# Attention in steps of two tiles: maximum, two score tiles, maximum, two mixes; GpSimd adds up eight or nine tiles of twelve

## The chip, the cores and the metric

The kernel runs on one core of one Trainium2 chip. The metric is the device time of one execution in microseconds; the time before is the median of three runs.

A core has five engines, each with its own stream of instructions: TensorE multiplies matrices (PE in the profile; PEld is its loading of weights), VectorE (DVE) and GpSimd (POOL) do elementwise work and VectorE reductions too, ScalarE (ACT) does activation functions and copies, and SyncE (SP) issues transfers. They run independently and wait for each other on semaphores only. Products land in PSUM; the rest lies in SBUF.

## The reference

Two transformer layers on `x`, 32 batches of 56 rows of 256, each with cross attention and then a mixture of experts. The change is in the attention alone. Its keys and values are the same 1500 rows of 64 of a batch (`ctx_512`) with rotary embedding; there are 16 heads. Per layer:

```
q_big = einsum('bshk,hkq->bshq', q_hk, w_kc_q)
kv_r = _apply_rope(kv_c, sin_k[None], cos_k[None])
q_r = einsum('bshq,hqr->bhsr', q_big, W_qr)
k_r = einsum('bld,hdr->bhlr', kv_r, W_kr)
scores = einsum('bhsr,bhlr->bhsl', q_r, k_r)
attn = softmax(scores, axis=-1)
ctx_c = einsum('bhsl,bld->bhsd', attn, kv_r)
ctx_lat = einsum('bhsd,hkd->bhsk', ctx_c, w_kc_kv)
```

## The kernel before

Each layer's attention goes through the 32 batches in four groups of eight (`BG`). A group begins with the projection of its queries (`qwide`, `query`); then come its batches one by one. The heads' queries are folded so that a batch has 896 query columns (16 heads of 56 rows), held as two halves of 448 on partitions 0 to 63 and 64 to 127; keys are held twice for that. The 1500 keys of a batch are 12 tiles of 125. The steps that matter, by the names that the schedule gives them:

- `smax` ("maximum"): a piece of the scores of a *later* batch (a quarter of the queries by a third of the keys), made only to find each query's maximum. TensorE writes it to the PSUM region `pair` (L853), VectorE reduces it to `maxpart` (L1120). A batch takes 12 of them, one for each tile of the batch before it. There is one `pair`, so a maximum is issued only when VectorE has drained the last one.
- `score`: a tile's scores in about full precision: `kparts` with `qhigh` (two products) and with `qlow` (L874), then the `shift` row that subtracts the maximum (L879). The two regions `wide` are taken in turn. ScalarE takes the exponential into `prob` (L975), which has four places.
- `mix`: `prob` times the values `kv` into one accumulator for the whole batch (L893). It is issued one tile late, after the next tile's scores. GpSimd adds the tiles' exponentials up in `sum_pool` (L1035, profile name `sums`) for the first `pool_tiles(b)` tiles; VectorE adds up the rest (L1141).
- `context`: after the last tile, ScalarE copies the accumulator (`ctx_raw`, L982) and VectorE adds its sum and GpSimd's (L1154).
- `norm`, `spread`, `share`: TensorE adds the sums over partitions (L900), ScalarE copies (`total`), the sums go by transfer to `packed`, VectorE takes the reciprocal (L1160), it goes to memory and back to all partitions (`zrec_merged`, `recip`), and VectorE multiplies (`ctx_n`, L1184).
- `maxneg`, `maxT`: the maxima of the next batch are reduced, transposed by TensorE (L859), copied by ScalarE and moved by transfer to `shift`; the first tile of the next batch waits for it.
- layer 0 only: `rotate` (GpSimd, L1007, L1008), `ropecos` (VectorE, `rope_c`, L1053), `rope` (VectorE, `kv`, L1063) and `keyT` (four transposes on TensorE, L811, a copy by ScalarE, a subtraction by VectorE to `kparts`, L1093) make the keys and values of a batch two or three ahead. Layer 1 fetches them.

`attention_schedule` writes all steps in one list, and every engine walks through that list and issues its part, waiting on semaphores. So the place of a step in the list is its place in the queue of every engine that takes part in it, SyncE's too.

Of the kernel before, what the change touches and what calls it, by code (L numbers as in the profile page):

```python
# [15 lines left out]
BG = 8  # L16
# [13 lines left out]
POOL_TILES, POOL_LAST = 11, 7  # L30
# [22 lines left out]
def pool_tiles(b):  # L53
    return POOL_TILES if b % BG < BG - 1 else POOL_LAST

def pool_sums(b):

    return sum(pool_tiles(i) - 1 for i in range(b))

def vector_sums(b):  # L60

    return sum(LT - pool_tiles(i) for i in range(b))

def attention_schedule(layer):
# [34 lines left out]
    for g in range(G):  # L99
        first, old = BG * g, BG * g - 1  # L100
        if layer == 0:
            for n in range(H + 1):
# [4 lines left out]
                if g and n == 0:  # L107
                    add("mix", old, LT - 1)
                    add("context", old)
# [39 lines left out]
        else:  # L149
            for p in range(NPAIR):  # L150
# [3 lines left out]
                if g and p == 0:  # L154
                    add("mix", old, LT - 1)
                    add("context", old)
# [26 lines left out]
        last = None  # L183
        for j in range(BG):
            b = first + j
            for t in range(LT):
                ahead = (j + 1, t + EARLY_MAX) if t + EARLY_MAX < LT else (j + 2, t + EARLY_MAX - LT)
# [4 lines left out]
                if layer == 0 and t == LT - 3 and b + 3 < NB:  # L192
                    add("rotate", b + 3)
# [24 lines left out]
                if layer == 0 and t >= LT - 2 and b + 3 < NB:  # L218
                    add("ropecos", b + 3, t - LT + 2)
                if layer == 0 and t in (1, 2) and b + 2 < NB:  # L220
                    add("rope", b + 2, t - 1)
                if g + 1 < G and j == BG - 2 and t == 4:
                    add("heads", g + 1)
                if g + 1 < G and j == BG - 1:
                    if t == 2:
                        add("mean", g + 1, region=3)
                    if t in (3, 4):
                        add("square", g + 1, t - 3)
                    if t == 5:
                        add("var", g + 1, region=3)  # L230
                    if t in (7, 8):
                        add("rstd", g + 1, t - 7)
                    if t == 9:
# [4 lines left out]
    add("mix", NB - 1, LT - 1)  # L238
# [373 lines left out]
def attention(nc, layer, a, scratch, x_all, sems, phase_range, sb, stack, region, c):  # L612
# [67 lines left out]
    with nc.Block() as block:  # L680
# [104 lines left out]
        def _(pe):  # L785
# [6 lines left out]
            for kind, key, reg in steps:  # L792
# [103 lines left out]
                elif kind == "norm":  # L896
                    b, = key
                    pe.wait_ge(s["dve_sum"], vector_sums(b + 1))
# [22 lines left out]
        def _(act):  # L921
            for kind, key, reg in steps:
# [40 lines left out]
                elif kind == "score":  # L963
# [3 lines left out]
                    if n_ >= NPROB:  # L967
# [3 lines left out]
                        if to < pool_tiles(bo):  # L971
                            act.wait_ge(s["pool_sum"], pool_sums(bo) + max(1, to))
                        else:
                            act.wait_ge(s["dve_sum"], vector_sums(bo) + max(1, to - pool_tiles(bo)))
# [16 lines left out]
        def _(pool):  # L991
            for kind, key, reg in steps:
# [16 lines left out]
                elif kind == "qrope":  # L1009
# [4 lines left out]
                    if g and h == 0:  # L1014
                        pool.wait_ge(s["dve_sum"], vector_sums(BG * g))
# [6 lines left out]
                elif kind == "mix":  # L1022
                    b, t = key
                    if 1 <= t < pool_tiles(b):
# [3 lines left out]
                        if t == 1:  # L1028
                            if b >= 2:
                                pool.wait_ge(s["dve_sum"], vector_sums(b - 1))  # L1030
                            first_in = prob[:, (n_ - 1) % NPROB, :]
                        else:
                            pool.wait_ge(s["pool_sum"], pool_sums(b) + t - 1)
# [4 lines left out]
        def _(dve):  # L1038
# [3 lines left out]
            for kind, key, reg in steps:  # L1042
# [52 lines left out]
                elif kind == "qrope":  # L1095
# [5 lines left out]
                    if g and h == 0:  # L1101

                        dve.wait_ge(s["premix"], LT * BG * g)
                        dve.wait_ge(s["pool_sum"], pool_sums(BG * g))
# [846 lines left out]
```

## Time and profile before

| | |
|---|---|
| median of three runs | 3254.75 us (3250.76 to 3263.74) |
| profiled execution, its own time | 3258.38 us |
| its span | 3256.6 us |
| TensorE, VectorE, ScalarE, GpSimd busy | 2906.2, 1959.9, 1184.5, 1660.3 us |
| layer 0's attention, about | 200 to 1460 us of the span |
| layer 1's attention, about | 1860 to 2900 us of the span |

The span is one profiled execution. An engine's busy share says how much it did, not what the others waited for; a busy TensorE can still be one that changes over between products. In the timeline, a line is one or several instructions of an engine, with what released it in brackets if the engine stood idle before.

### The profile page before, as it was taken

What the parts mean: (1) busy time and instruction counts of PE and PEld (TensorE: products, weight loads), DVE (VectorE), ACT (ScalarE), POOL (GpSimd) and SP (SyncE); (2) the same over time, 40 slices, a digit from 0 to 9 for tenths busy, and PEclk for the clock granted to TensorE, in tenths of its full rate; (3) what the DMA queues carried; (4) which work ended last, traced back from release to release, by engine and by line L of the source; (5) the groups of instructions that cost most, each with busy time, mean ns of one, the idle gap of its engine ahead of it and who ended that gap; (6) DMA issues with size and microseconds to landing.
All of it is one profiled execution on the core that took longest, in us unless ns stands there. A gap on an engine that the chain in (4) does not pass through costs nothing. (4 is left out here: it accounts for less than half of the span.)

```text
span 3256.6 us, 42708 instructions
## 1 busy us (share of the span) xinstructions
PE 2906.2 (89%) x15992; PEld 1650.1 (51%) x15992; DVE 1959.9 (60%) x2318; ACT 1184.5 (36%) x1644; POOL 1660.3 (51%) x947
## 2 busy tenths in 40 slices
PE   7689999998998999996899699899989989968888
PEld 6444444444544454445788444444444444436555
DVE  3476667666766676745766556556456566545553
ACT  3124441444144414443333244434424434422221
POOL 0367775776676657762100077567647737720000
PEclk9689999999999999998999799999999999988888
DMA  8333331333133413312000323223323313210000
GB/s 280 90 88 79 88 93 35 80 78 100 33 80 81 103 37 75 76 33 83 1 1 1 87 65 81 70 68 83 74 51 81 94 30 81 57 48 1 6 6 12
DMA packets 102326, 212.32 MB, mean 65 GB/s; under 512 B 30690, under 2 KB 77778, under 8 KB 94572
## 3 DMA queue, kind: packets, MB, share of 16 engines
q1 hardware_dynamic: 102124, 209.59, 24.8%
q8 instruction: 132, 2.16, 0.3%
q14 instruction: 70, 0.57, 0.1%
HBM read 138.51 MB, written 46.00 MB: 57 GB/s over the span
## 5 line engine op out<-in xcount | busy, mean ns | idle before, releaser
L1035 POOL TENSOR_TENSOR sums<-sums,prob 125x896 f32<-125x896 f32 x544 | 1148.2, 2111 | 207.9 <-ACT prob L975 160.6
L1120 DVE TENSOR_REDUCE maxpart<-pair 112x2 f32<-112x1000 f32 x720 | 861.0, 1196 | 468.4 <-PE pair L853 468.2
L975 ACT ACTIVATE prob<-wide 125x896 f32<-125x896 f32 x768 | 704.4, 917 | 874.0 <-PE wide L879 870.9
L893 PE MATMUL single<-prob,kv 125*64 125x448 f32 x3072 | 757.4, 572 | 0.7
L874 PE MATMUL wide<-qhigh,kparts 64*125 64x448 f32 x3072 | 455.0, 374 | 8.3 <-DVE maxpart L1120 8.3
L853 PE MATMUL pair<-kparts,qhigh 64*112 64x500 f32 x1440 | 349.4, 482 | 71.5 <-DVE maxpart L1120 70.3
L853 PEld LDWEIGHTS pair<-kparts,qhigh 64*112 64x112 f32 x1440 | 126.2, 172 | 493.1 <-DVE maxpart L1120 422.5
L1035 POOL TENSOR_TENSOR sums<-prob 125x896 f32<-125x896 f32 x64 | 134.7, 2105 | 457.9 <-ACT prob L975 457.9
L874 PEld LDWEIGHTS wide<-qhigh,kparts 64*125 64x125 f32 x3072 | 278.5, 184 | 116.5 <-issue 78.2
L879 PE MATMUL wide<-shift,ones_row 64*125 64x448 f32 x1536 | 286.1, 367 | 10.0 <-DMA shift<-maxrow 9.9
L874 PE MATMUL wide<-qlow,kparts 64*125 64x448 f32 x1536 | 284.2, 365 | 0.0
L893 PEld LDWEIGHTS single<-prob,kv 125*64 125x64 f32 x3072 | 153.2, 136 | 240.7 <-issue 235.5
L996 POOL TENSOR_TENSOR w_low<-w_low_values,w_high 128x384 fp32r<-128x384 f32 (+1 forms) x96 | 98.4, 1031 | 305.2 <-ACT w_high L941 305.2
L1752 POOL TENSOR_TENSOR ffn_hsum<-ffn_hid 128x448 f32<-128x448 f32 (+1 forms) x24 | 27.9, 1161 | 297.2 <-DVE ffn_hid L1878 297.2
L1020 POOL TENSOR_TENSOR sums<-prob 96x448 f32<-96x448 f32 x128 | 145.8, 1160 | 47.3 <-issue 24.1
L879 PEld LDWEIGHTS wide<-shift,ones_row 64*125 64x125 f32 x1536 | 145.4, 184 | 27.2 <-DMA shift<-maxrow 13.9
L874 PEld LDWEIGHTS wide<-qlow,kparts 64*125 64x125 f32 x1536 | 144.6, 184 | 13.6
L788 PE MATMUL wide<-x_high,w_high 128*96 128x448 f32 (+1 forms) x320 | 126.1, 394 | 21.3 <-POOL w_low L996 13.6
L1184 DVE TENSOR_TENSOR ctx_n<-ctx_raw,recip 128x448 f32<-128x448 f32 x62 | 91.2, 1472 | 84.2 <-DMA recip<-zrec_merged 84.2
L913 PE MATMUL wide<-ctx_n,wvo 128*128 128x448 f32 x256 | 121.5, 631 | 6.7 <-DVE ctx_n L1176 4.3
L1093 DVE TENSOR_TENSOR kparts<-single,kparts 64x500 fp32r<-64x500 f32 x94 | 63.0, 670 | 97.4 <-ACT kparts L948 97.4
L789 PE MATMUL wide<-x_high,w_low 128*96 128x448 f32 (+1 forms) x320 | 119.0, 372 | 0.0
(319 smaller groups left out, 3882.2 us busy)
## 6 DMA issues: line engine op xcount, KB each, us to landing
kparts<-keys_merged SPq DMA_DIRECT2D x64, 750.0 KB, 8.8
kparts<-kparts SPq DMA_DIRECT2D x96, 250.0 KB, 3.1
keys_merged<-kparts SPq DMA_DIRECT2D x32, 750.0 KB, 7.3
recip<-zrec_merged SPq DMA_DIRECT2D x124, 112.0 KB, 2.8
w_low_values<-w_merged SPq DMA_DIRECT2D x64, 192.0 KB, 2.4
raw<-in_ctx SPq DMA_DIRECT2D x32, 375.0 KB
values_merged<-kv SPq DMA_DIRECT2D x32, 375.0 KB
kv<-values_merged SPq DMA_DIRECT2D x32, 375.0 KB
```

Source lines behind the costliest of these rows:

```text
L788: pe.matmul(dst, w_hi, x_hi, start=start, stop=False)
L789: pe.matmul(dst, w_lo, x_hi, start=False, stop=False)
L853: mm = pe.matmul(acc[0:TQ, half, 0:LB], qhigh[rows_of(half), b % BG, t * TQ:(t + 1) * TQ], kparts[rows_of(half), b % 3, 0, third * LB:(thi ...
L874: pe.matmul(acc[0:LP, half, 0:HQ], kparts[rows_of(half), b % 3, part, cols], q[rows_of(half), b % BG, :], start=(i == 0), stop=False)
L879: mm = pe.matmul(acc[0:LP, half, 0:HQ], c["ones_row"][rows_of(half), 0:LP], shift[rows_of(half), b % 2, :], start=False, stop=True)
L893: mm = pe.matmul(mix_acc[64 * half:64 * half + DC, 0:HQ], kv[:, b % 3, t, :], prob[:, (b * LT + t) % NPROB, half * HQ:(half + 1) * HQ], st ...
L913: mm = pe.matmul(attn_acc[:, m, 0:NT].rearrange("p (j s) -> p j s", j=BG), wvo[:, i, m * 128:(m + 1) * 128], ctx_n[:, :, i * S:(i + 1) * S ...
L975: nc.scalar.activation(prob[:, n_ % NPROB, :].rearrange("p (a b) -> p a b", a=2), acc[0:LP, :, 0:HQ], ACT.Exp)\
L996: nc.gpsimd.tensor_tensor(w_low[:, h % HSLOT, :, :], w_in[:, h % HSLOT, :, :], w_high[:, h % HSLOT, :, :].bitcast(F32), ALU.subtract)\
L1020: nc.gpsimd.tensor_tensor(qr[:, h % 4, half, :], qa[:, h % 2, half, :], qb[:, h % 2, 1 - half, :], ALU.add)\
L1035: nc.gpsimd.tensor_tensor(dst, first_in, prob[:, n_ % NPROB, :], ALU.add).then_inc(s["pool_sum"], 1)
L1120: V.tensor_reduce(maxpart[:, b % 2, t:NMAX:4, third], acc[0:TQ, :, 0:LB], AX.X, ALU.max).then_inc(*R.signal_drained(kind, *key))
```

## The change

The loop over tiles becomes a loop over steps of two tiles. A step issues a maximum, both tiles' scores, a second maximum, and then both mixes of the step before. What hung on odd tiles moves: `norm` from tile 1 to step 2, `maxT` from tile 9 to step 8 (and so ahead of `spread` in the list), both `rope` adds to step 2, `keyT` from tiles 3, 4, 5 to steps 4, 6, 10, `rotate` to step 8, both `ropecos` and `stash` to step 10. VectorE's adding gets a kind of its own, `sum`, of the step's own tiles rather than at the mix. GpSimd takes 8 tiles in layer 0 and 9 in layer 1 where it took 11 (the last batch of a group keeps 7); VectorE takes the others.

```diff
-POOL_TILES, POOL_LAST = 11, 7
+POOL_TILES, POOL_LAST = (8, 9), 7
...
-            for t in range(LT):
-                ahead = (j + 1, t + EARLY_MAX) if t + EARLY_MAX < LT else (j + 2, t + EARLY_MAX - LT)
...
-                add("score", b, t, region=t % 2)
+            for t in range(0, LT, 2):
+
+                ahead = [(j + 1, u + EARLY_MAX) if u + EARLY_MAX < LT else (j + 2, u + EARLY_MAX - LT) for u in (t, t + 1)]
...
                 if j + 1 < BG and t == 8:
                     add("maxneg", b + 1)
-                if last is not None:
-                    add("mix", *last)
-                    if last[1] == LT - 1:
-                        add("context", last[0])
-                last = (b, t)
-                if t == 1 and j:
+                if ahead[0][0] < BG:
+                    maximum(first + ahead[0][0], ahead[0][1])
+                for u in (t, t + 1):
+                    add("score", b, u, region=u % 2)
+                if ahead[1][0] < BG:
+                    maximum(first + ahead[1][0], ahead[1][1])
+                if before is not None:
+                    for u in range(2):
+                        add("mix", before[0], before[1] + u)
+                    if before[1] == LT - 2:
+                        add("context", before[0])
+                before = (b, t)
+                for u in (t, t + 1):
+                    add("sum", b, u)
+                if t == 2 and j:
                     add("norm", b - 1, region=3)
-                if j + 1 < BG and t == 9:
+                if j + 1 < BG and t == 8:
                     add("maxT", b + 1, region=3)
-                if layer == 0 and t in (3, 4, 5) and b + 2 < NB:
-                    add("keyT", b + 2, t - 3, region=3)
-                if layer == 0 and t == LT - 1 and b + 2 < NB:
-                    add("stash", b + 2)
-                if ahead[0] < BG:
-                    maximum(first + ahead[0], ahead[1])
+                if layer == 0 and b + 2 < NB:
+                    places = (4, 6, 10) if j + 1 < BG else (6, 8, 10)
+                    if t in places:
+                        add("keyT", b + 2, places.index(t), region=3)
+                    if t == 10:
+                        add("stash", b + 2)
+                    if t == 2:
+                        for part in range(2):
+                            add("rope", b + 2, part)
+                if layer == 0 and b + 3 < NB:
+                    if t == 8:
+                        add("rotate", b + 3)
+                    if t == 10:
+                        for part in range(2):
+                            add("ropecos", b + 3, part)
                 if t == 8 and j:
                     add("spread", b - 1)
                 if t == 10 and j:
                     add("share", b - 1, 2)
```

In VectorE's stream, one batch in the middle of layer 0, from the sum of the batch before to that of this one, was this (`maxpart` are the reductions of maxima; an x2 is two in a row):

```order
L1154 TENSOR_TENSOR sums<-prob,sums 125x896
L1120 TENSOR_REDUCE maxpart<-pair 112x2 x2
L1063 TENSOR_TENSOR kv<-rope_c,rope_s 125x384
L1120 TENSOR_REDUCE maxpart<-pair 112x2
L1063 TENSOR_TENSOR kv<-rope_c,rope_s 125x384
L1093 TENSOR_TENSOR kparts<-single,kparts 64x500
...
L1160 RECIPROCAL packed_recip<-packed 112x8
L1120 TENSOR_REDUCE maxpart<-pair 112x2 x2
L1184 TENSOR_TENSOR ctx_n<-ctx_raw,recip 128x448
L1053 TENSOR_TENSOR rope_c<-raw,cosk 125x384
L1120 TENSOR_REDUCE maxpart<-pair 112x2
L1053 TENSOR_TENSOR rope_c<-raw,cosk 125x384
```

and becomes this:

```order
L1171 TENSOR_TENSOR sums<-sums 125x896
L1137 TENSOR_REDUCE maxpart<-pair 112x2 x2
L1080 TENSOR_TENSOR kv<-rope_c,rope_s 125x384 x2
L1137 TENSOR_REDUCE maxpart<-pair 112x2 x2
...
L1137 TENSOR_REDUCE maxpart<-pair 112x2 x2
L1158 TENSOR_TENSOR sums<-sums,prob 125x896 x2
L1110 TENSOR_TENSOR kparts<-single,kparts 64x500
L1070 TENSOR_TENSOR rope_c<-raw,cosk 125x384 x2
L1201 TENSOR_TENSOR ctx_n<-ctx_raw,recip 128x448
L1137 TENSOR_REDUCE maxpart<-pair 112x2 x2
```

The work between reductions is gathered behind every second one, and two `sums` join it at the batch's end.

TensorE's stream in layer 1, around the norm, was this (`single` takes the mixes and the norm):

```order
L879 MATMUL wide<-shift,ones_row 125x448 x2
L893 MATMUL single<-prob,kv 64x448 x2
L900 MATMUL single<-sums,ones 64x448 x2
L853 MATMUL pair<-kparts,qhigh 112x500 x2
L874 MATMUL wide<-qhigh,kparts 125x448 x4
L874 MATMUL wide<-qlow,kparts 125x448 x2
L879 MATMUL wide<-shift,ones_row 125x448 x2
L893 MATMUL single<-prob,kv 64x448 x2
L853 MATMUL pair<-kparts,qhigh 112x500 x2
```

and becomes this:

```order
L870 MATMUL pair<-kparts,qhigh 112x500 x2
L891 MATMUL wide<-qhigh,kparts 125x448 x4
L891 MATMUL wide<-qlow,kparts 125x448 x2
L896 MATMUL wide<-shift,ones_row 125x448 x2
L891 MATMUL wide<-qhigh,kparts 125x448 x4
L891 MATMUL wide<-qlow,kparts 125x448 x2
L896 MATMUL wide<-shift,ones_row 125x448 x2
L870 MATMUL pair<-kparts,qhigh 112x500 x2
L910 MATMUL single<-prob,kv 64x448 x4
L870 MATMUL pair<-kparts,qhigh 112x500 x2
```

Two tiles' scores stand between two maxima, and two mixes behind the second.

SyncE's transfers of a batch of layer 1 were in this order:

```order
L759 DMA packed<-total 56x1x8 x2
L736 DMA kparts<-keys_merged 64x3000 x2
L738 DMA kv<-values_merged 125x768
L763 DMA zrec_merged<-packed_recip 112x8
L768 DMA recip<-zrec_merged 64x448 x2
L777 DMA shift<-maxrow 1x4x112 x2
```

and become:

```order
L753 DMA kparts<-keys_merged 64x3000 x2
L755 DMA kv<-values_merged 125x768
L776 DMA packed<-total 56x1x8 x2
L794 DMA shift<-maxrow 1x4x112 x2
L780 DMA zrec_merged<-packed_recip 112x8
L785 DMA recip<-zrec_merged 64x448 x2
```

The shift transfers now stand ahead of those of the reciprocals.

## Rows read from the trace of the kernel before

**Rows 1.** The page, busy time and share of TensorE.

```profile
PE 2906.2 (89%) x15992; PEld 1650.1 (51%) x15992; DVE 1959.9 (60%) x2318; ACT 1184.5 (36%) x1644; POOL 1660.3 (51%) x947
```

**Rows 2.** Timeline, one tile of layer 1: start, length, engine, line, operation.

```profile
2217.64 0.48 PE L853 MATMUL pair<-kparts,qhigh 64*112 64x500 f32 x2
...
2217.83 20.08 POOL L1035 TENSOR_TENSOR sums<-sums,prob 125x896 f32<-125x896 f32 x9 [0.78 <-ACT prob L975]
...
2217.95 0.56 PE L874 MATMUL wide<-qhigh,kparts 64*125 64x448 f32 x4
2218.15 1.20 DVE L1120 TENSOR_REDUCE maxpart<-pair 112x2 f32<-112x1000 f32 x1 [0.94 <-PE pair L853]
...
2218.35 0.36 PE L874 MATMUL wide<-qlow,kparts 64*125 64x448 f32 x2
...
2218.55 0.37 PE L879 MATMUL wide<-shift,ones_row 64*125 64x448 f32 x2
...
2218.85 0.97 PE L893 MATMUL single<-prob,kv 125*64 125x448 f32 x4
2218.96 0.92 ACT L975 ACTIVATE prob<-wide 125x896 f32<-125x896 f32 x1 [1.21 <-PE wide L879]
...
2219.75 0.48 PE L853 MATMUL pair<-kparts,qhigh 64*112 64x500 f32 x2
```

**Rows 3.** Timeline, end of a batch in layer 1 and its norm.

```profile
2210.16 1.28 DVE L1184 TENSOR_TENSOR ctx_n<-ctx_raw,recip 128x448 f32<-128x448 f32 x1 [0.56 <-DMA recip<-zrec_merged]
...
2212.47 1.08 DVE L1154 TENSOR_TENSOR sums<-prob,sums 125x896 f32<-125x896 f32 x1
2212.61 0.48 PE L853 MATMUL pair<-kparts,qhigh 64*112 64x500 f32 x2 [0.40 <-DVE maxpart L1120]
...
2213.83 0.97 PE L893 MATMUL single<-prob,kv 125*64 125x448 f32 x4
...
2214.64 0.92 PE L900 MATMUL single<-sums,ones 125*64 125x448 f32 x4
...
2215.49 0.48 PE L853 MATMUL pair<-kparts,qhigh 64*112 64x500 f32 x2
```

**Rows 4.** Timeline, end of a batch in layer 0.

```profile
608.78 0.54 DVE L1053 TENSOR_TENSOR rope_c<-raw,cosk 125x384 f32<-125x384 f32 x1
...
610.49 0.48 PE L853 MATMUL pair<-kparts,qhigh 64*112 64x500 f32 x2 [1.97 <-DVE maxpart L1120]
```

**Rows 5.** Windows: stretch, length, busy per engine, granted clock, DMA share, GB/s.

```profile
611.40:614.80 3.40, 3.40 (x12) 0.77 (x8) 1.61 (x2) 0.92 (x1) 1.78 (x1) 0.50 0.31 79
...
579.30:768.00 188.70, 171.27 (x1102) 84.01 (x1102) 124.19 (x132) 83.59 (x108) 137.94 (x72) 0.98 0.33 84
```

**Rows 6.** Timeline, transfers of reciprocals and shift, and the shift's late landing.

```profile
2205.29 0.32 SPq L763 DMA_DIRECT2D zrec_merged<-packed_recip  x1
...
2207.82 1.35 SPq L777 DMA_DIRECT2D shift<-maxrow  x2
...
2320.09 0.62 DVE L1184 TENSOR_TENSOR ctx_n<-ctx_raw,recip 128x448 f32<-128x448 f32 x1 [8.87 <-DMA recip<-zrec_merged]
2320.10 0.46 PE L879 MATMUL wide<-shift,ones_row 64*125 64x448 f32 x2 [2.12 <-DMA shift<-maxrow]
```

**Rows 7.** Timeline, VectorE and GpSimd adding at once at the end of a group.

```profile
461.96 4.08 POOL L996 TENSOR_TENSOR w_low<-w_low_values,w_high 128x384 fp32r<-128x384 f32 x3 [1.95 <-ACT w_high L941]
...
462.44 1.43 DVE L1184 TENSOR_TENSOR ctx_n<-ctx_raw,recip 128x448 f32<-128x448 f32 x1
```

**Rows 8.** Timeline, key transposes in layer 0.

```profile
619.99 0.59 PE L811 MATMUL single<-ident,kv 125*64 125x125 f32 x4 [0.67 <-DVE kv L1063]
...
620.51 0.48 PE L853 MATMUL pair<-kparts,qhigh 64*112 64x500 f32 x2
...
621.23 0.67 DVE L1093 TENSOR_TENSOR kparts<-single,kparts 64x500 fp32r<-64x500 f32 x1 [1.39 <-ACT kparts L948]
...
621.83 1.18 DVE L1120 TENSOR_REDUCE maxpart<-pair 112x2 f32<-112x1000 f32 x1
```

More of the change, by code:

```diff
@@ L51, in head_at, with pool_tiles, pool_sums, vector_sums @@
     return n // 2 + n % 2 * NPAIR
[L53 to L62, printed above, removed]
+def pool_tiles(layer, b):
+    return POOL_TILES[layer] if b % BG < BG - 1 else POOL_LAST
+def pool_sums(layer, b):
+    return sum(pool_tiles(layer, i) - 1 for i in range(b))
+def vector_sums(layer, b):
+    return sum(LT - pool_tiles(layer, i) for i in range(b))
 def attention_schedule(layer):
@@ L107, in attention_schedule @@
                 if g and n == 0:
-                    add("mix", old, LT - 1)
+                    for u in range(2):
+                        add("mix", old, LT - 2 + u)
                     add("context", old)
@@ L154, in attention_schedule @@
                 if g and p == 0:
-                    add("mix", old, LT - 1)
+                    for u in range(2):
+                        add("mix", old, LT - 2 + u)
                     add("context", old)
@@ L203, in attention_schedule @@
-                last = (b, t)
-                if t == 1 and j:
+                if ahead[0][0] < BG:
[5 more added lines that the diff above has]
+                if before is not None:
+                    for u in range(2):
+                        add("mix", before[0], before[1] + u)
+                    if before[1] == LT - 2:
+                        add("context", before[0])
@@ L224, in attention_schedule @@
                 if g + 1 < G and j == BG - 1:
+                    if t == 0:
+                        add("mean", g + 1, region=3)
                     if t == 2:
[L226 to L229, printed above, removed]
+                        for k in range(KT):
+                            add("square", g + 1, k)
+                    if t == 4:
                         add("var", g + 1, region=3)
-                    if t in (7, 8):
-                        add("rstd", g + 1, t - 7)
-                    if t == 9:
+                    if t == 6:
+                        for part in range(2):
+                            add("rstd", g + 1, part)
+                    if t == 8:
                         add("xsplit", g + 1)
@@ L237, in attention_schedule @@
                             add("wsplit", g + 1, n)
-    add("mix", NB - 1, LT - 1)
+    for u in range(2):
+        add("mix", NB - 1, LT - 2 + u)
     add("context", NB - 1)
@@ L897, in _ @@
                     b, = key
-                    pe.wait_ge(s["dve_sum"], vector_sums(b + 1))
+                    pe.wait_ge(s["dve_sum"], vector_sums(layer, b + 1))
                     for half in range(2):
@@ L1014, in _ @@
                     if g and h == 0:
[L1015 removed]
+                        pool.wait_ge(s["dve_sum"], vector_sums(layer, BG * g))
                         pool.wait_ge(*R.filled("norm", BG * g - 1))
@@ L1023, in _ @@
                     b, t = key
-                    if 1 <= t < pool_tiles(b):
+                    if 1 <= t < pool_tiles(layer, b):
                         pool.wait_ge(*R.drained("score", b, t))
@@ L1127, in _ @@
                     V.tensor_reduce(maxneg[:, b % 2, 0:NMAX], maxpart[:, b % 2, :, :], AX.X, ALU.max, negate=True).then_inc(s["maxneg"], 1)
-                elif kind == "mix":
+                elif kind == "sum":
                     b, t = key
-                    if t > pool_tiles(b):
+                    if t > pool_tiles(layer, b):
                         n_ = b * LT + t
@@ L1133, in _ @@
                         dst = sum_dve
-                        if t == pool_tiles(b) + 1:
+                        if t == pool_tiles(layer, b) + 1:
                             if b:
@@ L1145, in _ @@
                     other = sum_dve
-                    if vector_sums(b + 1) - vector_sums(b) == 1:
+                    if vector_sums(layer, b + 1) - vector_sums(layer, b) == 1:
                         dve.wait_ge(*R.drained("score", b, LT - 1))
```

28 lines of the change are left out of this document (11 added, 17 removed).

## The prediction

> **What bounds the kernel now.** I read the page first: TensorE is busy 89% of the span [rows 1]. The page's share says nothing of which wait ends last, so I went to the timeline of the two attention stages, which hold 64 batches of 12 tiles. In one tile of layer 1 at full clock [rows 2] TensorE never stands idle: maximum to scores 0.31 us, scores 0.40 + 0.20, shift to mix 0.30, mix to the next maximum 0.90; a tile takes 2.11. Two of these steps are dearer than the streaming in them. A mix followed by work of its own shape hands over after 0.81 (2213.83 to 2214.64), and the norm, the same shape as a mix, hands over to a maximum after 0.85 [rows 3]. So each change between "64 rows at a time" products (maximum, scores) and "64 columns at a time" products (mix) costs time, and now there are two changes per tile.
>
> VectorE is the second thing to look at, because there is one maximum buffer: a maximum can be issued only when the reduction of the one before is done. The reduction starts 0.51 us after the maximum and takes 1.20 [rows 2], so a maximum is free 1.77 us after the last one, if VectorE does nothing else in between. At the end of a batch it does: `ctx_n` and `sums` stand between two reductions, and TensorE waits 0.40 us in layer 1 [rows 3] and 1.97 us in layer 0 [rows 4]. After that wait the granted clock is 0.50, that is 1.2 instead of 2.4 GHz, for 3.4 us [rows 5]. Over six batches of layer 0 the mean clock is 0.98 [rows 5].
>
> **TensorE's part of the change.** Per two tiles: 0.31, 0.60 (first scores), 0.20, 0.60 (second), 0.20, second maximum 0.31, first mix 0.81, second mix 0.85 = 3.88 us, against 4.22. The two handovers of 0.20 (scores to scores, scores to maximum) are not in the trace; I take the 0.20 between `qlow` and `shift` products of one shape [rows 2]. The other bound is 0.31, as from maximum to scores, which has the same shape too: then it is 4.10. Maximum to mix I take at 0.31 for the same reason. Saved: 0.34 us for each of the 320 two-tile steps that have maxima (40 of the 48 steps of each group of eight batches; the last eight have no batch left to look ahead to), -109 us; in the 64 without, twice 0.90 + 0.60 + 0.30 = 3.60 becomes 0.60 + 0.20 + 0.60 + 0.30 + 0.81 + 0.85 = 3.36, -15. Together -124 (bounds -46 and -124).
> The Trainium skill (TensorEngine Tiling, Key Properties) says that changing the tiling mode drains TensorE, while tiles within a mode run on. Rows 2 and 3 agree: 0.90 against 0.81. By that rule alone, with nothing else on the way, the sum would end here, at about 3,130 us.
>
> **VectorE's part.** The second maximum of a step is wanted 1.92 us after the first (0.31 + 0.60 + 0.20 + 0.60 + 0.20), the next step's first 1.96 us later. With a reduction of 1.20 starting 0.51 in, the free time between two reductions is 0.72 and 0.76 us. Everything else that VectorE does now stands in one of six places per batch, behind the second reduction of a step, and what is longer than about 0.9 us there holds TensorE up, since the maximum after next waits for it. Instructions follow each other 0.1 us before the profile's end of the one before, so a reduction counts 1.12, a lone `sums` (1.08 [rows 3]) 1.0; two that depend on each other count 2.1.
> *End of a batch, layer 1.* Counted from the first maximum of step 10: second reduction 2.43 to 3.55, two `sums` to 5.7, `ctx_n`, next reduction. `ctx_n` needs the reciprocals. From issue of `zrec_merged` (2205.29) to the start of `ctx_n` (2210.16) it is 4.87 us [rows 3, 6]; that issue now stands behind the two shift transfers, which take 1.35 to issue [rows 6] and wait for the maxT at the end of step 8. That puts the issue at 5.8 and `ctx_n` at 10.7 from the start of step 8, or 6.6 from step 10. Then `ctx_n` 0.54 (GpSimd has ended its eight sums by then), the reduction 7.1 to 8.3, and the maximum that was wanted at 5.8 goes at 8.4: a stall of 2.6 against 0.4 now, 20 times; 1.1 in each of 4 first batches, that have no `ctx_n`. +48 us.
> *End of a batch, layer 0.* Behind the reduction stand two `sums` (2.1), `kparts` (0.60 [rows 8]), two `rope_c` (0.47 each [rows 4]) and `ctx_n` (0.54): the next reduction starts at 7.75, the maximum wanted at 6.3 goes at 9.0. 2.7 against 1.97, 20 times, and 2.2 against nothing, 4 times: +23 us.
> *The two `kv` adds, layer 0, step 2.* They read two SBUF tensors, and so does GpSimd's sum. The timeline shows what these do to each other [rows 7]: of three `w_low` on GpSimd the first runs while `ctx_n` waits for it, the second only after `ctx_n`: 4.08 us for the three, and 1.43 for a `ctx_n` that takes 0.62 when GpSimd is not in the way [rows 6]. The first `kv` comes at 3.55. In step 2 GpSimd has tile 2 from 2.4 to 4.5 us and tile 3 ready behind it (tile 2's exponential ends at 0.91 + 0.41 + 0.92; sums go 20.08 / 9 = 2.23 apart [rows 2]). The first `kv` gets through at 4.9, GpSimd takes the next 2.1, the second `kv` ends at 7.4, and the maximum wanted at 6.5 goes at 8.6: 2.1 us, 27 batches, +57. What goes away is the 0.67 that the transposes waited for `kv` [rows 8], -18.
> *The key transposes in steps 4 and 6.* `kparts` starts 0.72 us after the maximum behind the transposes was issued and the reduction at 1.32 [rows 8] where 0.51 is usual; now the 2.11 us of a tile and the 0.52 of the transposes lie between that maximum and the next and hide it; with 1.92 between them 0.65 us show. 51 of them, +33.
> The Trainium skill (SBUF — State Buffer, on the shared port pair) says that VectorE and GpSimd hold this pair for a whole instruction and the other one fully blocks. Rows 7 show just that. It speaks against this change where it gives VectorE more adds of two SBUF tensors, 3 a batch instead of 1 in layer 1, but I find GpSimd idle at the places of those.
>
> **The clock.** Of the 20 waits of about 2.0 us that layer 0 has at ends of batches, the mean clock of 0.98 says that 8 or so were followed by a fall (0.02 / 0.5 x 189 us = 7.5 us at half clock per six batches, 3.4 us each [rows 5]). A fall costs 1.7 us. The changed kernel has 27 waits of 2.1 us and 40 of 2.6 or 2.7: at the same share 11 and 16 falls, 19 more than now, +32 (bounds 0, if waits in another rhythm cause no more than now, and +73, if each of the 40 causes one).
> **The shift row.** In batch 6 of a group the transfers of the next group's weights delay the reciprocals, and the shift transfer queued behind them lands late: TensorE waits 2.12 us [rows 6]. Now shift goes first. 6 times, -13.
> **GpSimd.** Sums are 2.23 apart [rows 2], more than the 1.94 a tile would take. With 7 or 8 of them per batch, not 10, it ends before the batch does; this I cost at nothing. With 10 it would set the pace.
>
> **Sum**, against the profiled execution (3258.4 us, span 3256.6): -124 + 48 + 23 + 57 - 18 + 33 + 32 - 13 = +38, so 3296; the median of the three runs is 3.6 below that execution, which gives 3293. The first term has a size of which I am sure within its bounds, the stalls in the few places that I could walk through; rounded, I forecast **3290 us**, 1.1% slower.
>
> **Rivals.**
> *Faster: the `kv` adds are not parted* (0.22). If GpSimd doesn't come between them, or if its third sum isn't ready, the second `kv` ends at 5.4 and the stall is 0.1. That takes 54 us and 11 falls (19 us) off: 3217. It decides the sign once fewer than half of the 27 batches show the second `kv` waiting. For it: VectorE's instructions follow without a gap, so VectorE may keep its place. Against: the turns in [rows 7].
> *No change: the clock stays* (0.25). All stalls come, yet TensorE falls no more often than now: 3258. For it: 12 of the 20 waits of 2.0 us had no fall behind them. Against: 8 had.
> *Slower still: GpSimd gets in before `ctx_n`* (0.10). Its first sum of the next batch becomes ready 0.4 us after `ctx_n` starts. If the reciprocals come later than that, `ctx_n` waits for a sum, 1.8 us in 40 batches: 3362. For it: a margin of 0.4 us at the end of a chain of 5. Against: that chain was steady enough for a wait of 0.56 only [rows 3].
> *The change doesn't do what it says* (0.08). Handovers within one shape cost 0.31: +78, 3368. For it: maximum to scores has one shape and costs 0.31. Against: `qlow` to `shift`, 0.20.
> *Forecast* (0.35): 3260 to 3320.
>
> "Faster", "same" and "slower" are parted at 0.5%, about what a measurement of this kernel can tell from no change (3238 and 3271). Faster: the first rival and a little of the second, 0.25. Same: the rest of the second and the low end of the forecast, 0.26. Slower 0.49. For eight in ten the range takes in the `kv` rival at its centre and leaves out most of the two dear ones: 3205 to 3335; the likeliest case alone is 3260 to 3320.
>
> **What would show it.** Right: two-tile steps of 3.9 us on TensorE with mixes 0.8 + 0.85; waits of the maximum for `maxpart` of 2.6 to 2.7 us once a batch and, in layer 0, of about 2 us after the `kv` adds, of which the second is some 2.5 us long; a lower mean clock in layer 0 than 0.98; no wait for `shift` in batch 6. Wrong: a second maximum that goes on time after `ctx_n`, layer 1 batches clearly under 26 us, `kv` adds of 0.55 back to back, or ScalarE waiting for sums, which would mean that GpSimd sets the pace after all.

## The result, and the profile after

The changed kernel takes 3320.34 us (median of 4 runs, 3316.98 to 3338.34), the kernel before, run on the same chip beside it, 3254.05 us (3250.76 to 3263.74). The ratio is 1.0209, 95% interval 1.0184 to 1.0233: slower by 2%, 66 us. Forecast were 3290 us and a range of 3205 to 3335, so the side and the range held; the size was 30 us short, 66 us of loss where some 35 were forecast, and the time lies at the upper end of the likeliest case (3260 to 3320).

The head of the page, and the page's first line on TensorE, answer to [rows 1]:

```profile
span 3316.0 us, 42706 instructions
...
PE 2844.9 (86%) x15992; PEld 1733.0 (52%) x15992; DVE 2145.9 (65%) x2458; ACT 1147.2 (35%) x1644; POOL 1369.1 (41%) x807
```

TensorE is busy 61.3 us less than before (2906.2), and the span is 59.4 us longer (3256.6 before): it stands idle for 471.1 us where it stood for 350.4. The clock hides a part of the saving. These are the views of the cores, first of before, then of after (span, mean granted clock):

```profile
core 0: 3256.6 us, clock 0.948
```

```profile
core 0: 3316.0 us, clock 0.932
```

The clock has only the levels 0.50 and 1.00 in these traces, so TensorE was at 1.2 GHz for (1 - 0.948) x 2 x 3256.6 = 339 us before and for (1 - 0.932) x 2 x 3316.0 = 451 us after. Half of the 112 us more, 56, is streaming that took twice as long. So the 59.4 us are made of three parts: 117 less work at full clock, 121 more idle, 56 lost to the clock. Not all of the last is the change's: 79 of the 112 us at half clock lie between the first and the last copy of an accumulator (`ctx_raw`) in each layer, 24 lie ahead of the first one (14 of these before any attention, in the first 200 us), and 10 behind the last one. In that first part the other kernels with the new order have between 3 us less and 29 us more than the one before, so how much of the 24 the change makes is open.

Whom TensorE waits for stands in the view of waits, after and, where the front shows none, before (line, releaser: total us, times, longest):

```profile
PE pair L870 <- DVE maxpart L1137: 221.8, 154, 4.8
```

```profile
PE pair L853 <- DVE maxpart L1120: 70.3, 84, 2.0
```

151 us of waiting for one reduction have come. Some 28 us of other waits have gone (19 for `kv`, 9 for `shift`), which leaves about the 121 us of idle time more. What stands between the reductions is seen in the timeline of the changed kernel, first at the end of a batch in layer 1, from the first maximum of the step before the last. It answers to [rows 2, 3]:

```profile
2252.86 0.48 PE L870 MATMUL pair<-kparts,qhigh 64*112 64x500 f32 x2
...
2254.79 0.39 PE L870 MATMUL pair<-kparts,qhigh 64*112 64x500 f32 x2
2255.11 0.20 PEld L910 LDWEIGHTS single<-prob,kv 125*64 125x64 f32 x4 [0.30 <-ACT prob L992]
...
2256.95 0.48 PE L870 MATMUL pair<-kparts,qhigh 64*112 64x500 f32 x2
...
2257.34 1.29 SPq L794 DMA_DIRECT2D shift<-maxrow  x2
...
2258.68 0.44 SPq L780 DMA_DIRECT2D zrec_merged<-packed_recip  x1
...
2260.45 1.08 DVE L1158 TENSOR_TENSOR sums<-prob 125x896 f32<-125x896 f32 x1
2260.87 0.17 PEld L870 LDWEIGHTS pair<-kparts,qhigh 64*112 64x112 f32 x2 [0.70 <-DVE maxpart L1137]
...
2261.63 1.09 DVE L1158 TENSOR_TENSOR sums<-sums,prob 125x896 f32<-125x896 f32 x1
...
2263.53 0.63 DVE L1201 TENSOR_TENSOR ctx_n<-ctx_raw,recip 128x448 f32<-128x448 f32 x1 [0.81 <-DMA recip<-zrec_merged]
2264.01 2.09 POOL L1052 TENSOR_TENSOR sums<-prob 125x896 f32<-125x896 f32 x1 [5.52 <-ACT prob L992]
2264.07 1.19 DVE L1137 TENSOR_REDUCE maxpart<-pair 112x2 f32<-112x1000 f32 x1
...
2265.32 0.48 PE L870 MATMUL pair<-kparts,qhigh 64*112 64x500 f32 x2 [2.35 <-DVE maxpart L1137]
```

`sums`, `sums`, a wait for the reciprocals, `ctx_n`, and only then the reduction: the maximum goes 2.35 us late. In 6 of the 20 such batches it is 4.76 us, and this is one of them:

```profile
2232.38 2.07 POOL L1052 TENSOR_TENSOR sums<-prob 125x896 f32<-125x896 f32 x1 [5.57 <-ACT prob L992]
2233.09 1.84 DVE L1201 TENSOR_TENSOR ctx_n<-ctx_raw,recip 128x448 f32<-128x448 f32 x1 [2.01 <-DMA recip<-zrec_merged]
2234.86 1.19 DVE L1137 TENSOR_REDUCE maxpart<-pair 112x2 f32<-112x1000 f32 x1
...
2236.10 0.76 PE L870 MATMUL pair<-kparts,qhigh 64*112 64x500 f32 x2 [4.76 <-DVE maxpart L1137]
2236.79 0.29 PEld L910 LDWEIGHTS single<-prob,kv 125*64 125x64 f32 x4 [0.43 <-issue]
2236.79 3.25 PE L910 MATMUL single<-prob,kv 125*64 125x448 f32 x8
```

The reciprocals landed 1.2 us later, GpSimd's first sum of the new batch got in 0.7 us ahead, and `ctx_n` took 1.84 us and not 0.63. Behind the gap the clock falls: the two mixes take 3.25 us and not 1.72.

In layer 0 the same view shows the end of a batch (to compare with [rows 4]), the `kv` adds and a key transpose ([rows 8]):

```profile
660.56 1.01 DVE L1070 TENSOR_TENSOR rope_c<-raw,cosk 125x384 f32<-125x384 f32 x2
...
661.49 0.61 DVE L1201 TENSOR_TENSOR ctx_n<-ctx_raw,recip 128x448 f32<-128x448 f32 x1
...
663.27 0.48 PE L870 MATMUL pair<-kparts,qhigh 64*112 64x500 f32 x2 [2.40 <-DVE maxpart L1137]
...
669.29 4.50 POOL L1052 TENSOR_TENSOR sums<-sums,prob 125x896 f32<-125x896 f32 x2 [5.25 <-ACT prob L992]
...
670.45 3.76 DVE L1080 TENSOR_TENSOR kv<-rope_c,rope_s 125x384 f32<-125x384 f32 x2
...
675.37 0.48 PE L870 MATMUL pair<-kparts,qhigh 64*112 64x500 f32 x2 [1.64 <-DVE maxpart L1137]
...
680.54 0.48 PE L870 MATMUL pair<-kparts,qhigh 64*112 64x500 f32 x2 [0.45 <-DVE maxpart L1137]
```

Two `kv` adds take 3.76 us: the first sits out the rest of the sum that GpSimd is at, the second the whole of the next one, which GpSimd begins between the two, as in [rows 7].

From one `ctx_raw` to the next a batch of layer 0 mostly takes 33.0 to 33.7 us (31.3 or 32.9 before), one of layer 1 some 27.2, or 31.0 with the long wait (26.9 before). The seventh of a group, which has none of these long waits now, takes 23.1 in layer 1 where it had 26.1 to 28.5.

### The profile page after: what moved, and what is told of

It reads as the page before. It is cut to its first block and busy times, and to the rows that moved or that the text cites. A ratio compares the mean times of both kernels' runs of the same rounds, so it can differ in the third digit from the quotient of the medians.

```text
span 3316.0 us, 42706 instructions
## 1 busy us (share of the span) xinstructions
PE 2844.9 (86%) x15992; PEld 1733.0 (52%) x15992; DVE 2145.9 (65%) x2458; ACT 1147.2 (35%) x1644; POOL 1369.1 (41%) x807
## 5 line engine op out<-in xcount | busy, mean ns | idle before, releaser
L1052 POOL TENSOR_TENSOR sums<-sums,prob 125x896 f32<-125x896 f32 x404 | 860.6, 2130 | 361.2 <-ACT prob L992 323.9
L992 ACT ACTIVATE prob<-wide 125x896 f32<-125x896 f32 x768 | 665.5, 917 | 478.3 <-PE wide L896 461.2
L910 PE MATMUL single<-prob,kv 125*64 125x448 f32 x3072 | 695.6, 576 | 0.0
L870 PE MATMUL pair<-kparts,qhigh 64*112 64x500 f32 x1440 | 339.5, 467 | 223.8 <-DVE maxpart L1137 221.8
L910 PEld LDWEIGHTS single<-prob,kv 125*64 125x64 f32 x3072 | 192.1, 140 | 302.2 <-issue 259.0
L891 PEld LDWEIGHTS wide<-qhigh,kparts 64*125 64x125 f32 x3072 | 288.2, 187 | 64.9 <-issue 30.6
L805 PE MATMUL wide<-x_high,w_high 128*96 128x448 f32 (+1 forms) x320 | 128.1, 400 | 26.1 <-POOL w_low L1013 19.5
L1158 DVE TENSOR_TENSOR sums<-sums,prob 125x896 f32<-125x896 f32 x108 | 121.2, 1122 | 14.2 <-ACT prob L992 6.0
L965 ACT ACTIVATE kparts<-single 64x500 fp32r<-64x500 f32 x94 | 54.7, 582 | 206.4 <-PE single L828 206.4
```

What stands on the lines that cost most here:

```text
L805: pe.matmul(dst, w_hi, x_hi, start=start, stop=False)
L870: mm = pe.matmul(acc[0:TQ, half, 0:LB], qhigh[rows_of(half), b % BG, t * TQ:(t + 1) * TQ], kparts[rows_of(half), b % 3, 0, third * LB:(thi ...
L891: pe.matmul(acc[0:LP, half, 0:HQ], kparts[rows_of(half), b % 3, part, cols], q[rows_of(half), b % BG, :], start=(i == 0), stop=False)
L910: mm = pe.matmul(mix_acc[64 * half:64 * half + DC, 0:HQ], kv[:, b % 3, t, :], prob[:, (b * LT + t) % NPROB, half * HQ:(half + 1) * HQ], st ...
L992: nc.scalar.activation(prob[:, n_ % NPROB, :].rearrange("p (a b) -> p a b", a=2), acc[0:LP, :, 0:HQ], ACT.Exp)\
L1052: nc.gpsimd.tensor_tensor(dst, first_in, prob[:, n_ % NPROB, :], ALU.add).then_inc(s["pool_sum"], 1)
```

## The experiments

**Theory A**: the new order puts all of VectorE's other work behind every second reduction, where it adds up and meets GpSimd's sums, and the maxima pay for it. **Theory B**: VectorE has too much to do, because GpSimd sums eight or nine tiles and not eleven. Each of the eleven kernels was timed against the kernel before on the same chip (3249 to 3254 us); where two of them are compared in microseconds they can come from different chips, and a few microseconds can be that.

**1. The new order, GpSimd at eleven tiles.**

```diff
-POOL_TILES, POOL_LAST = (8, 9), 7
+POOL_TILES, POOL_LAST = (11, 11), 7
```

> The two-tile steps with GpSimd adding up 11 tiles in both layers, as before the change. Theory A (the new order gathers VectorE's work behind every second reduction, and that holds the maxima up; moving sums to VectorE is only a part of it): the two sums leave the end of the batch, but GpSimd is then busy where rope_c and ctx_n stand, which have to take turns with it; layer 1 still waits for the reciprocals at the same place. About the same as the changed kernel or some 1% slower, 3320 to 3350 us. Theory B (VectorE was given too many sums, and the order by itself is good): faster than before, under 3240 us.

Measured: 3313.36 us, ratio 1.0184 (1.0164 to 1.0203). Nearly all of the loss is there with VectorE relieved of the sums, and the 7 us less are not clear of noise (the two intervals overlap):

```profile
PE pair L870 <- DVE maxpart L1137: 214.9, 152, 4.8
```

**2. One tile at a time as before, with the new split of the sums.** The schedule function is the one of before; each sum stands beside its mix.

> The one-tile order of before with the sums divided as in the changed kernel, 8 and 9 tiles on GpSimd. Theory A: the sums of 1.0 us each stand between reductions that have 0.9 us to spare, and GpSimd is idle at the end of a batch, so that ctx_n gets shorter: within 1% of before, 3250 to 3285 us. Theory B: most of the loss is here, 3300 us or more.

Measured: 3271.37 us, ratio 1.006 (1.0042 to 1.0077). The maxima wait no longer than before (66.1 us), but the norm does, for VectorE's last sum (8.2 us before):

```profile
PE pair L857 <- DVE maxpart L1124: 66.1, 84, 2.0
...
PE single L904 <- DVE sums L1158: 26.2, 33, 3.3
```

So the split of the sums costs 0.6% in the old order, and B is not the cause of the 2%.

**3. The changed kernel with the `kv` adds in steps 2 and 4, behind the step's work, and the transposes two steps later.**

```diff
-                    places = (4, 6, 10) if j + 1 < BG else (6, 8, 10)
+                    places = (6, 8, 10)
...
-                    if t == 2:
-                        for part in range(2):
-                            add("rope", b + 2, part)
+                    if t in (2, 4):
+                        add("rope", b + 2, t // 2 - 1)
```

> The changed kernel with the two kv adds of layer 0 in steps 2 and 4 rather than both in step 2, and the key transposes in steps 6, 8, 10. Theory A: the second kv no longer waits for a turn of GpSimd ahead of a reduction; the wait of 1.6 us behind it goes in 27 batches, -45 to -50 us: about 3270 us. Theory B: layer 0's loss is the sums', and the wait shows up elsewhere: over 3300 us.

Measured: 3442.53 us, ratio 1.0587 (1.0565 to 1.0609). A miss of mine: the maxima of that batch begin in step 8, and their keys are doubled by a transfer that starts only behind the transposes. Once a batch a maximum now waits some 4.55 us for it, which the timeline and the waits show:

```profile
621.55 0.76 PE L869 MATMUL pair<-kparts,qhigh 64*112 64x500 f32 x2 [4.55 <-DMA kparts<-kparts]
```

```profile
PE pair L869 <- DVE maxpart L1136: 187.1, 102, 4.8
PE pair L869 <- DMA kparts<-kparts: 109.1, 24, 4.6
```

It says nothing for or against A, except that waits for `maxpart` fell by 35 us.

**4. `ctx_n` of two batches back, in step 0, between the scores and the second maximum.** In layer 0 its reciprocals have mostly landed by then, in layer 1 only just.

```diff
+                if t == 0 and j >= 2:
+                    add("share", b - 2, 2)
...
-                if t == 10 and j:
+                if t == 10 and j == BG - 1:
                     add("share", b - 1, 2)
```

> The changed kernel with ctx_n moved from the end of step 10 to step 0 of the next batch, between its two reductions, where the reciprocals have landed and GpSimd has not begun. Theory A: layer 1's waits of 2.35 and 4.75 us at the ends of batches fall to about 1 us, layer 0's from 2.4 to under 2, and fewer falls of the clock follow: -60 to -75 us, about 3250 us. Theory B: -10 to -15 us, the 0.54 of ctx_n itself in 20 batches.

Measured: 3272.93 us, ratio 1.0063 (1.0047 to 1.0078), 47 us less than the changed kernel. A regular batch's end in layer 1 now waits 0.92 us, and no wait of 4.76 is left. The gain is layer 1's: from its first to its last `ctx_raw` it takes 940 us where it took 979. Layer 0 has as much idle time as in the changed kernel (153 us), since in its step 0 GpSimd is adding, and `ctx_n` mostly takes some 2.5 us:

```profile
659.97 2.46 DVE L1203 TENSOR_TENSOR ctx_n<-ctx_raw,recip 128x448 f32<-128x448 f32 x1
```

**5. The `kv` adds apart, each between a step's two reductions, the transposes where the change has them.**

```diff
                 for u in (t, t + 1):
                     add("score", b, u, region=u % 2)
+                if layer == 0 and t in (2, 4) and b + 2 < NB:
+                    add("rope", b + 2, t // 2 - 1)
...
-                    if t == 2:
-                        for part in range(2):
-                            add("rope", b + 2, part)
```

> The changed kernel (3320) with the two kv adds of layer 0 parted: one in step 2 and one in step 4, each between the scores and the second maximum, so that VectorE takes it between its two reductions; keys keep their places. Theory A (VectorE's work gathered behind the second reduction holds the maxima up): the 1.6 us stall behind the pair of adds goes in 30 batches of layer 0 (-48), and a part comes back where the second reduction of the step is late (0.3 twice a batch, +18): 3275 to 3300. Theory B (only VectorE's total counts, which is unchanged): 3320.

Measured: 3252.2 us (10 runs, 3241.46 to 3264.84), ratio 1.0004 (0.9989 to 1.002): 68 us less than the changed kernel, with the same instructions. The timeline shows the two adds:

```profile
663.78 0.55 DVE L1079 TENSOR_TENSOR kv<-rope_c,rope_s 125x384 f32<-125x384 f32 x1
...
664.44 4.35 POOL L1051 TENSOR_TENSOR sums<-sums,prob 125x896 f32<-125x896 f32 x2 [3.63 <-ACT prob L991]
...
668.42 0.79 DVE L1079 TENSOR_TENSOR kv<-rope_c,rope_s 125x384 f32<-125x384 f32 x1
...
669.11 8.85 POOL L1051 TENSOR_TENSOR sums<-sums,prob 125x896 f32<-125x896 f32 x4 [0.32 <-ACT prob L991]
```

0.55 and 0.79 us in place of 3.76 for the pair: at the first GpSimd has a pause, and the second starts 0.37 us before a sum of GpSimd's ends (664.44 + 4.35), behind which it has one. The time is 23 us below the range that A gave. TensorE's idle time between the first and the last `ctx_raw` of layer 0 fell by 47 us as expected (153 to 106), and it was at half speed for 65 us there and not 99, which is another 17 us.

**6, 7, 8. Both moves; both with eleven tiles; `ctx_n` alone with eleven tiles.** The edits are those of 4 and 5 and of 1.

> The kv adds parted as in the run before, and ctx_n of a batch put two batches on, between the scores and the second maximum of step 0. Theory A: the two gains add (-45 measured for ctx_n alone, -20 to -45 for the adds): 3230 to 3260, about the kernel before. Theory B: as with ctx_n alone, 3273, since the adds only change places.

> Both moves, and GpSimd sums eleven tiles again in both layers. Theory A: VectorE has two or three adds less (1.1 us each) per batch behind the reductions of steps 8 and 10, where they meet the reciprocal: the wait of 0.92 at a layer 1 batch's end goes to 0.3 or less, that at layer 0's from 1.9 to 1.0: 3200 to 3235, faster than the kernel before. Theory B (too many adds on VectorE): also faster than the run with both moves and eight or nine tiles, by more, since all adds are off VectorE: below 3200. Rival C (GpSimd's last add, 2 us each, is now the late one, and norm waits for it): no better than with both moves, 3250 or more.

> Only ctx_n put two batches on, with GpSimd at eleven tiles. Tells the share of the kv adds from that of the sums. Theory A: the run with ctx_n alone (3273) less the 7 us that eleven tiles gave in the changed kernel, and less the end waits that sums and reciprocal still make: 3245 to 3268. Theory C: 3273 or more.

Measured: 3219.43 us (ratio 0.9905, 0.9884 to 0.9926), 3185.57 us (0.9802, 0.9785 to 0.9819) and 3243.16 us (0.9979, 0.9962 to 0.9995). The moves nearly add, as A has it: 47 and 68 us apart, 101 together, with every sum where the change put it, which B doesn't allow. But all three are faster than A's ranges by 2 to 14 us, and the 3186 of the second is inside what I had written for B. Read together they say that the sums matter once the moves are made: they are then what stands behind the last reductions of a batch, and eleven tiles on GpSimd give 34 us with both moves and 30 with `ctx_n`'s alone, where they gave 7 in the first experiment. C falls for the seventh: TensorE waits nowhere for GpSimd's last add.

**9. The seventh with `ctx_n` in step 6 and not in step 0.**

```diff
-                if t == 0 and j >= 2:
+                if t == 6 and j >= 2:
                     add("share", b - 2, 2)
```

> The run with both moves and eleven tiles (3186), with ctx_n of two batches back in step 6 and not in step 0. There its trace shows at a regular end in layer 1 ctx_n, then a reduction, then the 1.91 us add of the two sums, and behind it a reduction for which TensorE waits 0.42 and 0.80; in layer 0 0.44, 0.52, 1.38 and 0.37 a batch. Theory A (what meets in one slot behind a reduction is what holds TensorE up): the 1.2 us of the end of a layer 1 batch mostly go, 20 times, and about as much in layer 0: 3145 to 3170. Theory B (VectorE's total, unchanged): 3186.

Measured: 3159.71 us (3154.39 to 3167.94), ratio 0.9725 (0.9692 to 0.9757). It is inside A's range, 26 us less than the seventh, and the fastest of all. Part of the gain is that `ctx_n` needs no longer wait: in step 6 its reciprocals have landed 13 us or more before in a regular batch, and it takes 0.61 us there, where in step 0 it waited about 0.9 us for them in layer 1. Head of its page, and the view of waits:

```profile
PE 2791.0 (89%) x15992; PEld 1715.7 (54%) x15992; DVE 1973.5 (63%) x2318; ACT 1149.9 (36%) x1644; POOL 1703.9 (54%) x947
```

```profile
PE pair L871 <- DVE maxpart L1138: 115.3, 122, 2.0
```

A batch of layer 0 takes 29.2 us, one of layer 1 24.4 at the start of a group and 26.4 or 28 from the fourth of a group on. The timeline tells why:

```profile
2158.37 2.11 POOL L1053 TENSOR_TENSOR sums<-sums,prob 125x896 f32<-125x896 f32 x1
2160.43 2.13 POOL L1053 TENSOR_TENSOR sums<-prob 125x896 f32<-125x896 f32 x1
2160.61 2.89 DVE L1172 TENSOR_TENSOR sums<-prob,sums 125x896 f32<-125x896 f32 x1
...
2164.67 0.48 PE L871 MATMUL pair<-kparts,qhigh 64*112 64x500 f32 x2 [1.68 <-DVE maxpart L1138]
```

VectorE's last add needs GpSimd's last sum, which ends at 2160.48, and it starts 0.13 us behind that. By then GpSimd began its next sum 0.18 us ago, and the add takes 2.89 us for 1.08. So GpSimd, with ten sums 2.25 us apart in a batch of 24.4 us, has become the late one here. Behind the seventh batch of a group, where VectorE has little else to do, the view of waits names it:

```profile
DVE sums L1172 <- POOL sums L1053: 58.1, 5, 11.9
```

**10. The old order with only `ctx_n` two batches back, in step 6.**

```diff
+                if t == 6 and j >= 2:
+                    add("share", b - 2, 2)
-                if t == 10 and j:
+                if t == 10 and j == BG - 1:
                     add("share", b - 1, 2)
```

> The kernel before (3252) in its one-tile order, with only ctx_n put two batches on, into step 6, and the sums as they were. Tells whether the moves that repair the two-tile order would serve the old one as well. Theory A: the old order hands VectorE a reduction every tile with little else behind each, its waits at a batch's end are 0.4 us or less in layer 1, so the move is worth at most 0.4 x 44 = 18 us: 3235 to 3255. If it gave 50 us or more, ctx_n's place would be the gain in the other runs and not what the new order makes of it.

Measured: 3197.27 us (3185.88 to 3202.28), ratio 0.9827 (0.9796 to 0.9858). 52 us, where I had reckoned with 18 at most. I had counted 0.4 us for 44 ends and forgotten layer 0, where [rows 4] have 1.97. The kernel before's timeline shows what made that wait, and the new one's what became of it:

```profile
606.36 2.50 DVE L1184 TENSOR_TENSOR ctx_n<-ctx_raw,recip 128x448 f32<-128x448 f32 x1 [0.43 <-DMA recip<-zrec_merged]
```

```profile
611.02 0.72 DVE L1186 TENSOR_TENSOR ctx_n<-ctx_raw,recip 128x448 f32<-128x448 f32 x1
```

```profile
PE pair L855 <- DVE maxpart L1122: 25.6, 44, 2.0
```

The 1.97 us were thus made mostly by `ctx_n` meeting a sum of GpSimd's (2.50 us for 0.72), less by its wait for the reciprocals (0.43 us). So the place of `ctx_n` cost the old order some 50 us as well. By the condition that I had set (50 us or more), its gain isn't one that the new order owes: in the comparison of orders it has to stand on both sides. With `ctx_n` put right in both, the new order (0.9725) is 1% faster than the old (0.9827), 33 to 38 us. That gain lies in layer 1, where the stretch from the first to the last `ctx_raw` takes 927 us and not 965; a regular batch of layer 0 takes 29.2 us in the one and 29.3 in the other.

**11. The ninth with the change's own eight and nine tiles.** The edit is the first one backwards.

> The changed kernel with only the two moves (kv adds parted into steps 2 and 4, ctx_n two batches back in step 6) and its own eight or nine tiles on GpSimd. Beside the run with eleven tiles (3160) it prices the second half of the change where nothing else is late. Theory A: the two or three adds more per batch stand behind the reductions of the last steps and hold one maximum up by 0.3 to 1.0 us a batch: 3175 to 3200. Rival B (GpSimd's first sum no longer gets in front of VectorE's last add, 1.7 us in 16 batches of layer 1, so fewer tiles pay): 3130 to 3155.

Measured: 3181.68 us (3176.4 to 3185.42), ratio 0.9774 (0.9758 to 0.979), 22 us more than with eleven tiles (16 by the two ratios), inside A's range; rival B falls. In the best order found, too, taking sums from GpSimd costs time. It does drive off GpSimd's early turn in layer 1 (TensorE waits 0.92 us there, 22 times, where it waited 1.66, 16 times), but at the end of a batch in layer 0 it waits 1.9 us, 23 times, where it waited 1.4. By layers, nine tiles cost 4 us in layer 1 (931 for 927) and eight cost 25 in layer 0 (1168 for 1143); eleven in layer 0 and nine or ten in layer 1 was not tried.

## Why the prediction was right, and where its sum was off

The sum said +38 us and the profiled execution shows +59. Term by term, with waits counted in the trace:

| term | predicted | measured |
|---|---|---|
| TensorE's work at full clock | -124 | -117 |
| end of a batch, layer 1 | +48 | +59 |
| end of a batch, layer 0 | +23 | +19 |
| `kv` adds, and the transposes' wait gone | +57 - 18 | +44 - 19 |
| key transposes, steps 4 and 6 | +33 | +14 |
| `shift` in batch 6 | -13 | -9 |
| idle time elsewhere | 0 | +13 |
| clock, in the two attention stages | +32 | +40 |
| clock, elsewhere | 0 | +16 |

- *TensorE's part* held. A step of two tiles is 3.92 us (2248.94 to 2252.86 in layer 1), forecast 3.88, and the handovers of 0.20 which no row had shown were there: the second tile's scores start 0.21 after the first tile's `shift`, the second maximum 0.20 after the second one's. The rival "the change doesn't do what it says" falls. The rule of the Trainium skill (TensorEngine Tiling, Key Properties) that a change of tiling mode drains TensorE agrees with that: with half as many changes the 48 steps of a group went faster by about the expected amount.
- *End of a batch, layer 1.* The walk through it came out to 0.1 us: `ctx_n` 6.6 us after the first maximum of step 10 (2256.95 to 2263.53), a wait of 2.35 us for 2.6, 14 times 2.3 to 2.7. What was missing in it is the third rival, which I had given 0.10: GpSimd's first sum was ready 0.5 us after `ctx_n` started, and in 6 batches of 20 it was first. Those cost 28.5 us of waits. At the ends of layer 0's batches this never happened. Why the reciprocals land 1.2 us later in some batches I have not found out.
- *End of a batch, layer 0*: 2.41 us, 20 times, for 2.7, and 1.9, 4 times, for 2.2.
- *The `kv` adds* were parted by GpSimd in 26 of the 27 batches, as the turns of [rows 7] had said (in the very first they took 0.55 us each, and nothing waited); 1.6 us, 23 times, and 2.4 in the first batches of three groups, for 2.1. The first rival falls. The rule of the Trainium skill (SBUF — State Buffer, on the shared port pair), that the engine which starts first keeps the pair for its whole instruction, agrees with the rows above: 3.76 us for the two `kv`, 1.84 and 2.50 for `ctx_n`, 2.89 for the last add.
- *The key transposes* showed 0.45 and 0.53 us for 0.65, 52 times, and I had not taken off the 0.35 us that one of three had cost before, 30 times.
- *The clock*: 112 us more of half clock where the sum had 19 falls of 3.4 us, 65 us. Of the 112, 41 lie in layer 0's attention and 38 in layer 1's; the other 33, 16 us of time, lie outside, and no term of the sum could have had them. Inside, the number of falls was right and their place was not. Counted in the trace, 28 of the 70 long waits have a fall in or just behind them, against 8 of 19 before, about the share that was assumed. But the 26 waits behind the `kv` adds have 2 and not 11, and the 44 at ends of batches have 26 and not 16: 16 of 20 of the 2.41 us in layer 0, all 6 of 4.76 us in layer 1, 2 of the 14 shorter ones there. That the sum of the two came out is luck. The measured 56 lies inside the bounds of 0 and 73 that I gave. The second rival (the clock stays) falls.
- *Idle time elsewhere*, for one part the beginnings of the groups, where I had walked through nothing. There TensorE waits 5.9 us more for `w_low` and 3.3 us more for `x_n`.
- *GpSimd.* "With 10 it would set the pace" was wrong for the changed kernel, as its twin with ten sums shows (experiment 1). The pace of 2.23 us a sum was read rightly (2.10 of work and 0.14 between two), but it stood against the time of a tile, and a batch has ten sums in twelve tiles: 22.5 us, in batches of 27. It comes true only in the ninth run, where layer 1's batches are down to 24.4 us. What eight or nine tiles cost is 0.6% in the old order and 22 to 34 us in the repaired new one; no run shows a gain by them.

The terms' errors go both ways: the `kv` adds, the key transposes and layer 0's ends were priced 37 us too dear; layer 1's ends, the clock, the idle time elsewhere, the `shift` and TensorE's saving came out 59 us worse than priced. That the sum missed by no more than 21 us is in part luck.

So: slower for the reason given, that work gathered behind every second reduction holds the maxima up for more than the halved changes of shape save. Experiments 4 and 5 show it directly: with the same instructions in other places, 47 and 68 us come back, and together 101. What I argued only, and no run isolates, is how much of a gain is the clock's: its share is an estimate from the granted clock of one execution of each kernel.

## What to carry to other kernels

When an order is made coarser to save handovers on one engine, list for the engine that drains its single buffer what now stands between two drains, and move each piece into the slot that has a pause; the order here lost 2% as it was written, and gained 2.7% with two pieces moved and the split of the sums taken back. An operation that ends a chain of transfers, as `ctx_n` does, should be issued where its input has long landed and, if it adds or multiplies two SBUF tensors, where GpSimd doesn't stand in its way or nobody waits behind it: that alone was worth 1.7% in the kernel before. When batches get shorter, the engine that was far from late can become the late one (GpSimd in the ninth run). And look up when the moved input is next needed (experiment 3), since the transposes two steps later cost 3.7%.

## What the runs showed that I had not expected

- The same VectorE add of two SBUF tensors takes 0.55 to 0.79 us or, the pair of them, 3.76, by nothing but its place against GpSimd's sums; one `ctx_n` took 0.63, 1.84 or 2.50 us.
- GpSimd gets a turn between two adds of VectorE that stand one behind the other (669.29 beside 670.45), so that two short adds in a row cost up to two of GpSimd's sums.
- The clock does not go by the length of a wait alone: 16 of 20 waits of 2.41 us at layer 0's ends had a fall behind them, 2 of 14 waits of 2.3 to 2.7 us at layer 1's, and none of 23 of 1.6 us. Why, no run tells.
- The cost of idle gaps is more than the gaps: the changed kernel stands idle for 121 us more, and pays another 56 in lower clock, 40 of them in the attention stages. In experiment 5, 47 us of idle time less in layer 0 went with a layer 0 that was 72 us shorter.
- The old order holds its clock best: 0.952 in the second and the tenth run, against 0.945 in the ninth, which is shorter.
